# The row maxima of a pair attention: one transpose and four masked copies in place of four transposes and one copy

## The chip, the core and the metric

The kernel runs on one core of a Trainium2 chip. A core has five engines with instruction queues of their own: TensorE (PE; its weight loads are shown as PEld), VectorE (DVE), ScalarE (ACT), GpSimd (POOL) and SyncE (SP), which only starts transfers here. They meet through semaphores. SBUF is the core's memory of 128 partitions, PSUM the smaller one that TensorE writes (8 banks of 512 float32 per partition). The metric is the device time of one execution in microseconds, as a median over several.

## The reference

Two layers on x of shape (2, 1024, 128), each adding an attention, a feed-forward, another attention and another feed-forward to x. Only the attentions over 16 heads of 64 are touched. In one layer's terms:

```python
x = x + _L0_attn_a_ref(_layernorm(x), ...)   # no mask; one key and value head shared by all
x = x + _L0_ffn_ref(_layernorm(x), ...)      # both operands rounded to an FP6 grid
x = x + _L0_attn_b_ref(_layernorm(x), ...)   # causal, keys and values per head
x = x + _L0_ffn_ref(_layernorm(x), ...)
x = x + _L1_attn_a_ref(_layernorm(x), ...)   # causal, keys and values from a latent of 32
x = x + _L1_ffn_ref(_layernorm(x), ...)      # 8 experts, top 2, and a shared one
x = x + _L1_attn_b_ref(_layernorm(x), ...)   # causal, with biases
x = x + _L1_ffn_ref(_layernorm(x), ...)
```

and one attention is

```python
sim = jnp.einsum('bnhk,bmk->bnhm', q, k) / jnp.sqrt(KEY_DIM)
attn = jax.nn.softmax(sim, axis=-1)
o = jnp.einsum('bnhm,bmv->bnhv', attn, v)
out = jnp.einsum('bnhv,dhv->bnd', o, output_proj)
```

## The kernel before, in words

The program is a row of phases. `stream_phase` holds the first two attentions (the non-causal one from 75 to about 760 us, the causal one to about 1410) with the norm and feed-forward between them woven in; `latent_phase` is the third attention and has its own code, which the change doesn't touch; `attention_phase` is the last one (2010 to 2590). The first two and the last are "pair attentions": an item is one batch and two heads, head 0 on partitions 0 to 63 and head 1 on 64 to 127. An item has two units, its halves of 512 queries (`part` or `s`), and a unit has steps, one for each tile of 128 keys. There are 32 items in the stream and 16 in the last attention, so 96 units.

The softmax subtracts the row maximum before the exponential, and the scores are laid out with keys on partitions and queries along the free dimension. So the maxima are found first, from scores in the other layout:

- `chunk` (TensorE, L1010 and L530) makes scores with 128 queries on partitions, up to 512 keys of both heads, in PSUM banks 4 and 5.
- `row_max` (VectorE, L1210 and L697) reduces them to two numbers per partition, negated. Where a tile of queries has over 512 keys, the two halves go to `half_max`, and after the unit's last chunk a TENSOR_TENSOR takes their minimum into `neg_max` (L1217, L704). Where it has not, they go straight to `neg_max`. The buffer `neg_max` holds, for each half, four tiles of 128 columns, zero but for columns 0 and 64 of each, the two heads.
- `top` (TensorE, L1060 and L570) transposes the four tiles into the four quarters of PSUM bank 7, called `small`: the maxima of 512 queries now lie along the free dimension, on row 0 for head 0 and row 64 for head 1, zeros on all others.
- ScalarE copies the bank into `max_row` (L1146, L658).
- `scores` (TensorE, L986 and L989, L506 and L509) adds, to the product of keys and queries, the product of `pick` with `max_row`. The constant `pick` has ones in rows 0 and 64, so it spreads the maxima over the 128 keys.
- ScalarE takes the exponential (L1114, L621), GpSimd adds the tiles of it up (`add_up`, L1371, L781), TensorE multiplies with the values (`mix_step`, L1029, L549), and from the sums comes "total" (L1064, L574), a matmul with ones into the same bank `small`; VectorE inverts and multiplies (L1230, L1238), and "out" (L1069, L582) projects into `small` again.

The order is written out by hand. Every engine walks the steps `g` in pairs; `when` says at which step each use of `small` stands. Each use on TensorE first waits until the one before it has been copied out (`small_out`), and `scores` of a unit's first step waits for the copy of its "top". In a non-causal item (16 steps) the uses stand at 14 (top of half 0, for the next item), 1, 2, 3, 4, 6 (top of half 1), 10 and 11. In a causal item (12 steps) they stand at every step but two, and each top (steps 6 and 2) is followed at the very next step by a "total", with two calls of `mix_step` between them. Chunks run ten steps ahead of the scores.

Of the kernel before, what the change touches and what calls it, by code (L numbers as in the profile page):

```python
# [27 lines left out]
P = 128  # L28
# [53 lines left out]
def setup_phase(nc, m, a, dram):  # L82

    with phase(nc) as (ctx, sem):
# [40 lines left out]
        @block.gpsimd  # L125
        def _(pool):
            pool.memset(m.ident[:], 0.0).then_inc(zeroed, 1)
            pool.memset(a.shifted_ident[:], 0.0).then_inc(zeroed, 1)
            pool.memset(a.causal[:], 0.0).then_inc(zeroed, 1)
            pool.memset(m.earlier[:], 1.0).then_inc(zeroed, 1)  # L130
            pool.memset(ones, 1.0).then_inc(zeroed, 1)
            pool.memset(rows_of_ones, 0.0).then_inc(zeroed, 1)
            pool.memset(m.ones_row[:], 1.0).then_inc(zeroed, 1)
            pool.memset(a.ones[:], 1.0).then_inc(zeroed, 1)
            pool.memset(a.neg_max[:], 0.0).then_inc(zeroed, 1)
            pool.wait_ge(zeroed, 9)
            pool.affine_select(out=m.ident[:], in_=m.ident[:], compare_op=ALU.not_equal, fill=1.0, base=0,
                               pattern=[[-1, P]], channel_multiplier=1).then_inc(consts, 1)
            pool.affine_select(out=m.earlier[:], in_=m.earlier[:], compare_op=ALU.is_gt, fill=0.0, base=0,
                               pattern=[[1, EXPERTS], [-1, EXPERTS]], channel_multiplier=0).then_inc(consts, 1)  # L140
            for n, half in enumerate((slice(0, HD), slice(HD, P))):
                pool.wait_ge(consts, 2 + 3 * n)
                pool.affine_select(out=rows_of_ones[half], in_=rows_of_ones[half], compare_op=ALU.not_equal,
                                   fill=1.0, base=0, pattern=[[0, P]], channel_multiplier=1).then_inc(consts, 1)
                pool.affine_select(out=a.shifted_ident[half], in_=a.shifted_ident[half], compare_op=ALU.not_equal,
                                   fill=1.0, base=0, pattern=[[HD, 2], [-1, P]], channel_multiplier=1)\
                    .then_inc(consts, 1)
                pool.affine_select(out=a.causal[half], in_=a.causal[half], compare_op=ALU.is_ge, fill=MASKED, base=0,
                                   pattern=[[HD, 2], [-1, P]], channel_multiplier=1).then_inc(consts, 1)

            rows = (slice(0, LOW), slice(LOW, LOW + EXPERTS))
            done = 8
            for base, sign in ((0, 1), (ED - 1, -1)):
                for part in rows:
                    pool.wait_ge(consts, done)
                    pool.affine_select(out=ones[part], in_=ones[part], compare_op=ALU.is_ge, fill=0.0, base=base,
                                       pattern=[[sign, EXPERTS * ED]], channel_multiplier=-sign * ED)\
                        .then_inc(consts, 1)  # L160
                    done += 1
# [221 lines left out]
def attention_phase(nc, m, a, tag, dram, after, causal, biased=False, shared=False):  # L383
# [5 lines left out]
    with phase(nc) as (ctx, new_sem):  # L389
# [106 lines left out]
        def _(pe):  # L496
# [57 lines left out]
            def use_small(n, kind, i, part):  # L554
# [11 lines left out]
                                                w.v[:, 0 if shared else i // B, :], start=True, stop=True)  # L566
                elif kind == "top":
                    pe.wait_ge(max_ready, unit(i, part) + 1)
                    for t in range(TPG):
                        last = nc.tensor.transpose(small[:, t * P:(t + 1) * P], a.neg_max[:, part, t, :], m.ident[:])  # L570
                elif kind == "total":
                    pe.wait_ge(summed, sums_done[end_step(i, part) - 1])
                    for head, rows in enumerate(HEADS):
# [37 lines left out]
        def _(act):  # L611
# [19 lines left out]
            def take_small(n, kind, i, part):  # L631
# [23 lines left out]
                elif kind == "top":  # L655
                    if i >= 1:
                        act.wait_ge(scored, end_step(i - 1, part))
                    last = act.activation(a.max_row[:, part, :], small, ACT.Copy)  # L658
                else:
                    if unit(i, part) >= 1:  # L660
                        act.wait_ge(inverted, QUARTERS * unit(i, part))
                    last = act.activation(a.total[:], small, ACT.Copy)  # L662
# [19 lines left out]
        def _(dve):  # L682
            v = nc.vector

            def row_max(c):
# [3 lines left out]
                if split_max[s]:  # L689
                    out = a.half_max[:, part, t % TPG, :]  # L690
                    if part == 0 and t % TPG == 0 and unit(i, s) > 0:
                        dve.wait_ge(max_ready, unit(i, s))
                else:
                    out = a.neg_max[:, s, t % TPG, 0:P:HD]
                    if t % TPG == 0 and i >= 1:
                        dve.wait_ge(small_mm, use_of["top", i - 1, s] + 1)
                last = v.tensor_reduce(out, chunk_ps[:, :, 0:hi - lo], AX.X, ALU.max, negate=True)  # L697
                last.then_inc(maxed, 1)
                if c % NS == last_chunk[s]:
                    if split_max[s]:  # L700
                        if i >= 1:
                            dve.wait_ge(small_mm, use_of["top", i - 1, s] + 1)
                        dve.wait_ge(maxed, c + 1)
                        v.tensor_tensor(a.neg_max[:, s, :, 0:P:HD], a.half_max[:, 0], a.half_max[:, 1], ALU.min)\  # L704
                            .then_inc(max_ready, 1)
                    else:
                        dve.wait_ge(maxed, c + 1)
# [83 lines left out]
def shape_constants(nc, pool, a, sem):  # L791


    blank, shaped = sem("blank"), sem("shaped")
    for buffer, value in ((a.later[:], 0.0), (a.tri_scores[:], 0.0), (a.tri_chunk[:], 0.0), (a.unit32[:], 0.0), (a.pick4_raw, 0.0)):
        pool.memset(buffer, value).then_inc(blank, 1)
    pool.wait_ge(blank, 5)
    for rows in (slice(0, HD), slice(HD, P)):
        pool.affine_select(out=a.later[rows], in_=a.later[rows], compare_op=ALU.is_ge, fill=MASKED, base=0,
                           pattern=[[-HD, 2], [1, P]], channel_multiplier=-1).then_inc(shaped, 1)  # L800
    pool.wait_ge(shaped, 2)
    for rows in QUADRANTS:
        pool.affine_select(out=a.tri_scores[rows], in_=a.tri_scores[rows], compare_op=ALU.is_ge, fill=MASKED, base=0,
                           pattern=[[LATENT, 4], [-1, P]], channel_multiplier=1).then_inc(shaped, 1)
# [3 lines left out]
                           pattern=[[-1, LATENT]], channel_multiplier=1).then_inc(shaped, 1)  # L808
        pool.affine_select(out=a.pick4_raw[rows], in_=a.pick4_raw[rows], compare_op=ALU.not_equal, fill=1.0, base=0,
                           pattern=[[0, P]], channel_multiplier=1).then_inc(shaped, 1)  # L810
    pool.wait_ge(shaped, 18)
    pool.tensor_copy(a.pick4[:], a.pick4_raw).then_inc(shaped, 1)


def stream_phase(nc, m, a, dram, after):
# [6 lines left out]
    with phase(nc) as (ctx, new_sem):  # L822
# [153 lines left out]
        def _(pe):  # L976
# [73 lines left out]
            def use_small(n, kind, i, part):  # L1050
# [5 lines left out]
                    last = values(i, part)  # L1056
                elif kind == "top":
                    pe.wait_ge(max_ready, unit(i, part) + 1)
                    for t in range(TPG):
                        last = nc.tensor.transpose(small[:, t * P:(t + 1) * P], a.neg_max[:, part, t, :], m.ident[:])  # L1060
                elif kind == "total":
                    pe.wait_ge(summed, sums_done[end_step(i, part) - 1])
                    for head, rows in enumerate(HEADS):
# [40 lines left out]
        def _(act):  # L1104
# [19 lines left out]
            def take_small(n, kind, i, part):  # L1124
# [18 lines left out]
                elif kind == "top":  # L1143
                    if i >= 1:
                        act.wait_ge(scored, end_step(i - 1, part))
                    last = act.activation(a.max_row[:, part, :], small, ACT.Copy)  # L1146
                elif kind == "total":
                    if unit(i, part) >= 1:
                        act.wait_ge(inverted, QUARTERS * unit(i, part))
# [43 lines left out]
        def _(dve):  # L1193
# [3 lines left out]
            def row_max(c):  # L1197
# [6 lines left out]
                    if part == 0 and t % TPG == 0 and unit(i, s) > 0:  # L1204
                        dve.wait_ge(max_ready, unit(i, s))
                else:
                    out = a.neg_max[:, s, t % TPG, 0:P:HD]
                    if t % TPG == 0 and i >= 1:
                        dve.wait_ge(small_mm, use_of["top", i - 1, s] + 1)
                last = v.tensor_reduce(out, chunk_ps[:, :, 0:hi - lo], AX.X, ALU.max, negate=True)  # L1210
# [2 lines left out]
                if ends and split:  # L1213
                    if i >= 1:
                        dve.wait_ge(small_mm, use_of["top", i - 1, s] + 1)
                    dve.wait_ge(maxed, c + 1)
                    v.tensor_tensor(a.neg_max[:, s, :, 0:P:HD], a.half_max[:, 0], a.half_max[:, 1], ALU.min)\  # L1217
                        .then_inc(max_ready, 1)
                elif ends:
                    dve.wait_ge(maxed, c + 1)  # L1220
# [678 lines left out]
def build(nc, dram, out):  # L1899
    with ExitStack() as ctx:  # L1900
# [34 lines left out]
        a.unit32 = sb("unit32", [P, LATENT], BF16)  # L1935
        a.pick4_raw, a.pick4 = m.scratch[:, 7 * S:7 * S + P], sb("pick4", [P, P], F32R)
        a.later = sb("later", [P, 2, P], BF16)
        a.half_max = sb("half_max", [P, 2, TPG, 2])
        a.max_row = sb("max_row", [P, 2, BANK], F32R)
        a.mixed_raw = sb("mixed_raw", [P, 2, BANK])  # L1940
# [67 lines left out]
```

## Time and profile before

| | us |
|---|---|
| median of 3 timed runs | 2740.98 (2740.84 to 2741.83) |
| profiled execution | 2724.3 |
| its span | 2722.6 |
| TensorE busy | 2496.9 (92%) |
| VectorE busy | 1702.5 (63%) |
| ScalarE busy | 1159.5 (43%) |
| GpSimd busy | 1238.3 (45%) |

The span is from the first to the last instruction of the profiled execution; the time of the execution holds 1.7 us more around it. Shares are over the whole span, and the stages differ: the page's 40 slices show TensorE at nine tenths or more in all slices but those at the start and around the norms and feed-forwards. The mean granted clock of TensorE is 0.957 of full speed. Matmuls are pipelined and their ends are modelled, so that starts are the safer numbers for them.

### The profile page before, as it was taken

How to read it: one execution, taken by the hardware profiler on the slowest of the kernel's cores; microseconds unless marked ns; L12 is line 12 of the kernel's file. 1: busy time of each engine (PE TensorE's matmuls, PEld its weight loads, DVE VectorE, ACT ScalarE, POOL GpSimd, SP SyncE). 2: the span in 40 equal slices, each digit the busy share in tenths (PEclk: the TensorE clock that was granted, in tenths of full speed). 3: DMA queues.
4: the chain of work that ended last, by engine and by line, in shares of the span. 5: the costliest groups of instructions: out<-in, count | busy, mean ns of one | idle time of the engine just before them, and what ended most of it. 6: DMA issues, size and time to landing. Idle time of an engine off the chain costs nothing. (4 is left out here: it accounts for less than half of the span.)

```text
span 2722.6 us, 48683 instructions
## 1 busy us (share of the span) xinstructions
PE 2496.9 (92%) x20217; PEld 1321.3 (49%) x20217; DVE 1702.5 (63%) x2156; ACT 1159.5 (43%) x1526; POOL 1238.3 (45%) x809
## 2 busy tenths in 40 slices
PE   4999999999999999999994799997869999999969
PEld 2344444344444454555552566665535555555535
DVE  2577767877765766666657476764435566666644
ACT  2444444445444435444442244444124444444432
POOL 2577777766775535555550000000005455555520
PEclk9999999999999999999995799998879999999979
DMA  4000000000000000000000000000000000000000
GB/s 106 1 1 1 0 1 1 1 1 1 1 1 10 1 1 1 1 1 1 1 1 11 21 3 3 3 3 2 0 1 1 1 1 1 1 1 1 1 0 16
DMA packets 19183, 14.08 MB, mean 5 GB/s; under 512 B 3090, under 2 KB 17811, under 8 KB 18836
## 3 DMA queue, kind: packets, MB, share of 16 engines
q1 hardware_dynamic: 18964, 10.97, 1.6%
q8 instruction: 161, 2.64, 0.4%
q14 instruction: 58, 0.48, 0.1%
HBM read 9.39 MB, written 1.57 MB: 4 GB/s over the span
## 5 line engine op out<-in xcount | busy, mean ns | idle before, releaser
L1371 POOL TENSOR_TENSOR sums<-sums,p 128x1024 f32<-128x1024 f32 (+3 forms) x384 | 815.3, 2123 | 386.0 <-PE ps L1029 344.1
L1210 DVE TENSOR_REDUCE half_max<-ps 128x2 f32<-128x1024 f32 (+3 forms) x384 | 439.6, 1145 | 330.3 <-PE ps L1010 317.9
L1114 ACT ACTIVATE p<-ps 128x1024 f32<-128x1024 f32 (+3 forms) x384 | 347.5, 917 | 212.2 <-PE ps L989 153.0
L986 PE MATMUL ps<-q,k 64*128 64x512 f32 (+3 forms) x1792 | 425.2, 553 | 0.0
L781 POOL TENSOR_TENSOR sums<-sums,p 128x1024 f32<-128x1024 f32 (+3 forms) x160 | 277.1, 1732 | 198.5 <-PE ps L549 182.1
L1029 PE MATMUL ps<-p,v 128*64 128x512 f32 (+3 forms) x1536 | 338.7, 555 | 0.0
L989 PE MATMUL ps<-max_row,pick 64*128 64x512 f32 (+3 forms) x896 | 325.6, 723 | 0.0
L1230 DVE RECIPROCAL inverse<-total 128x128 f32<-128x128 f32 x256 | 239.9, 940 | 15.9 <-ACT total L1150 12.3
L1010 PE MATMUL ps<-k_near,q_near 64*128 64x512 f32 (+2 forms) x896 | 199.8, 442 | 40.0 <-DVE half_max L1210 39.9
L697 DVE TENSOR_REDUCE half_max<-ps 128x2 f32<-128x1024 f32 (+3 forms) x128 | 129.3, 1010 | 123.1 <-PE ps L530 109.3
L1590 ACT ACTIVATE p<-ps 128x2048 f32<-128x2048 f32 (+1 forms) x80 | 136.6, 1708 | 161.7 <-PE ps L1493 90.7
L1010 PEld LDWEIGHTS ps<-k_near,q_near 64*128 64x128 f32 x896 | 85.3, 187 | 246.2 <-issue 148.3
L986 PEld LDWEIGHTS ps<-q,k 64*128 64x128 f32 x1792 | 161.9, 187 | 55.9 <-issue 40.9
L1029 PEld LDWEIGHTS ps<-p,v 128*64 128x64 f32 x1536 | 97.0, 137 | 177.7 <-issue 112.4
L1643 DVE TENSOR_REDUCE quarter_max<-ps 128x2 f32<-128x1024 f32 (+3 forms) x128 | 128.2, 1012 | 59.8 <-PE ps L1517 34.2
L506 PE MATMUL ps<-q,k 64*128 64x512 f32 (+3 forms) x768 | 163.6, 504 | 0.0
L621 ACT ACTIVATE p<-ps 128x1024 f32<-128x1024 f32 (+3 forms) x160 | 118.7, 768 | 68.5 <-PE ps L514 52.0
L717 DVE RECIPROCAL inverse<-total 128x128 f32<-128x128 f32 x128 | 119.6, 940 | 15.8 <-ACT total L662 12.3
L989 PEld LDWEIGHTS ps<-max_row,pick 64*128 64x128 f32 x896 | 85.1, 187 | 89.8 <-issue 84.7
L1705 POOL TENSOR_TENSOR mixed<-mixed_raw,inverse 128x256 f32<-128x256 f32 x32 | 23.3, 727 | 229.7 <-DVE inverse L1661 229.7
L509 PE MATMUL ps<-max_row,pick 64*128 64x512 f32 (+3 forms) x384 | 121.5, 629 | 0.0
L549 PE MATMUL ps<-p,v 128*64 128x512 f32 (+3 forms) x640 | 115.7, 474 | 0.0
(252 smaller groups left out, 3990.9 us busy)
## 6 DMA issues: line engine op xcount, KB each, us to landing
q_w<-in_wq SPq DMA_DIRECT2D x3, 512.0 KB
o_w<-in_wo SPq DMA_DIRECT2D x3, 512.0 KB
k_w<-in_wk SPq DMA_DIRECT2D x2, 512.0 KB
v_w<-in_wv SPq DMA_DIRECT2D x2, 512.0 KB
out<-x SPq DMA_DIRECT2D x4, 256.0 KB, 2.9
scratch<-in_wq_t SPq DMA_DIRECT2D x1, 512.0 KB, 5.4
scratch<-in_w_out SPq DMA_DIRECT2D x1, 512.0 KB, 7.7
gate<-in_gate SPq DMA_DIRECT2D x1, 320.0 KB
```

The source lines that it names most:

```text
L506: nc.tensor.matmul(out[:, head, 0:width], a.k[rows, key_slot(i, 3), k * P:(k + 1) * P], a.q[rows, i % 3, s * BANK + lo:(s + 1) * BANK], st ...
L697: last = v.tensor_reduce(out, chunk_ps[:, :, 0:hi - lo], AX.X, ALU.max, negate=True)
L781: pool.tensor_tensor(sums, sums, probabilities(g)[:, :, lo:BANK], ALU.add).then_inc(summed, 1)
L986: nc.tensor.matmul(out[:, head, 0:width], a.k[rows, owner(i) % 3, k * P:(k + 1) * P], a.q[rows, i % 3, s * BANK + lo:(s + 1) * BANK], star ...
L989: last = nc.tensor.matmul(out[:, head, 0:width], a.pick[rows, :], a.max_row[rows, s, lo:BANK], start=False, stop=not diagonal)
L1010: last = nc.tensor.matmul(chunk_ps[:, head, 0:hi - lo], a.q_near[rows, i % 2, t * P:(t + 1) * P], a.k_near[rows, owner(i) % 2, lo:hi], sta ...
L1029: last = nc.tensor.matmul(mix[rows, lo:BANK], a.v[:, owner(i) % 2, k, value_columns(i, head)], probabilities(g)[:, head, lo:BANK], start=k ...
L1114: act.activation(probabilities(g)[:, :, lo:BANK], score[g % 2][:, :, 0:BANK - lo], ACT.Exp)\
L1210: last = v.tensor_reduce(out, chunk_ps[:, :, 0:hi - lo], AX.X, ALU.max, negate=True)
L1230: v.reciprocal(a.inverse[:, cols], a.total[:, cols]).then_inc(inverted, 1)
L1371: pool.tensor_tensor(sums, sums, probabilities(g)[:, :, lo:BANK], ALU.add).then_inc(summed, 1)
L1590: act.activation(probs[:, g % SLOTS, :, 0:width(s, n)], score[:, :, 0:width(s, n)], ACT.Exp)\
```

## The change

Four things are changed, in both pair phases alike.

- `neg_max`: the maxima of tile t now go to columns t and 64 + t of the first tile alone, so one transpose gives rows 0 to 3 (head 0) and 64 to 67 (head 1), each row the maxima of one tile.
- The spreading: ScalarE makes four copies of the same 128 columns, one into each quarter of `max_row`, with the scale taken from column t of a new constant `row_mask` [128 x 4], which is 1 on rows t and 64 + t and 0 elsewhere. All other rows become 0.
- `pick` has ones in rows 0 to 3 and 64 to 67, where only the row of the right tile is not zero.
- The minimum of the halves is a TENSOR_REDUCE over the last axis of one reordered view of `half_max`, in place of a TENSOR_TENSOR of its two halves.

```diff
@@ setup_phase
-                pool.affine_select(out=rows_of_ones[half], in_=rows_of_ones[half], compare_op=ALU.not_equal,
-                                   fill=1.0, base=0, pattern=[[0, P]], channel_multiplier=1).then_inc(consts, 1)
+                pool.affine_select(out=rows_of_ones[half], in_=rows_of_ones[half], compare_op=ALU.is_ge,
+                                   fill=1.0, base=-TPG, pattern=[[0, P]], channel_multiplier=1).then_inc(consts, 1)
@@ use_small, on TensorE (stream_phase; attention_phase has the same)
                     pe.wait_ge(max_ready, unit(i, part) + 1)
-                    for t in range(TPG):
-                        last = nc.tensor.transpose(small[:, t * P:(t + 1) * P], a.neg_max[:, part, t, :], m.ident[:])
+                    last = nc.tensor.transpose(small[:, 0:P], a.neg_max[:, part, 0, :], m.ident[:])
@@ take_small, on ScalarE
                     if i >= 1:
                         act.wait_ge(scored, end_step(i - 1, part))
-                    last = act.activation(a.max_row[:, part, :], small, ACT.Copy)
+                    for t in range(TPG):
+                        last = act.activation(a.max_row[:, part, t * P:(t + 1) * P], small[:, 0:P], ACT.Copy,
+                                              scale=a.row_mask[:, t:t + 1])
@@ row_max, on VectorE
-                    out = a.neg_max[:, s, t % TPG, 0:P:HD]
+                    out = a.neg_max[:, s, 0, t % TPG:P:HD]
...
-                    v.tensor_tensor(a.neg_max[:, s, :, 0:P:HD], a.half_max[:, 0], a.half_max[:, 1], ALU.min)\
+                    v.tensor_reduce(a.neg_max[:, s, 0, :].rearrange("p (h t) -> p t h", h=2)[:, 0:TPG, :],
+                                    a.half_max[:].rearrange("p a t h -> p t h a"), AX.X, ALU.min)\
                         .then_inc(max_ready, 1)
@@ shape_constants, on GpSimd, at the start of the stream
-    for buffer, value in ((a.later[:], 0.0), (a.tri_scores[:], 0.0), ...
+    for buffer, value in ((a.row_mask[:], 0.0), (a.later[:], 0.0), (a.tri_scores[:], 0.0), ...
...
     for rows in (slice(0, HD), slice(HD, P)):
+        pool.affine_select(out=a.row_mask[rows], in_=a.row_mask[rows], compare_op=ALU.not_equal, fill=1.0, base=0,
+                           pattern=[[-1, TPG]], channel_multiplier=1).then_inc(shaped, 1)
@@ build
+        a.row_mask = sb("row_mask", [P, TPG])
```

No instruction changes its place among the others; the counts at a top do. On TensorE, around a top in the non-causal part (line numbers of the changed kernel differ by a few). Before, and then changed:

```order
L1010 MATMUL ps<-k_near,q_near 128x512 x2
L1060 MATMUL ps<-ident,neg_max 128x128 x4
L1029 MATMUL ps<-p,v 64x512 x4
L1010 MATMUL ps<-k_near,q_near 128x512 x2
L986 MATMUL ps<-q,k 128x512 x2
```

```order
L1014 MATMUL ps<-k_near,q_near 128x512 x2
L1063 MATMUL ps<-ident,neg_max 128x128
L1033 MATMUL ps<-p,v 64x512 x4
L1014 MATMUL ps<-k_near,q_near 128x512 x2
L990 MATMUL ps<-q,k 128x512 x2
```

Behind the top stand the mixes and the next chunk. Where four transposes stood there is one; the chunk ahead of it, the mixes behind it and the chunk and scores that follow are the same. On ScalarE, around a top in the non-causal part, before and then changed:

```order
L1114 ACTIVATE p<-ps 128x1024 x2
L1146 ACTIVATE max_row<-ps 128x512
L1114 ACTIVATE sums<-ps 128x1024
L1114 ACTIVATE p<-ps 128x1024
L1122 ACTIVATE mixed_raw<-ps 128x512
```

```order
L1117 ACTIVATE p<-ps 128x1024 x2
L1150 ACTIVATE max_row<-ps,row_mask 128x128 x4
L1117 ACTIVATE sums<-ps 128x1024
L1117 ACTIVATE p<-ps 128x1024
L1125 ACTIVATE mixed_raw<-ps 128x512
```

The copy of 512 columns has become four of 128 that read `row_mask` too, in the same place between the exponentials of two units.

## Rows read from the trace of the kernel before

**Rows 1.** busy time by stage: us, then each engine (instructions); PEclk, DMA share, GB/s
```profile
75.00:1410.00 1335.00, 1293.32 (x7814) 609.84 (x7816) 916.23 (x986) 619.65 (x811) 856.06 (x472) 0.99 0.01 1
2070.00:2560.00 490.00, 486.35 (x3606) 254.51 (x3602) 306.06 (x339) 227.84 (x327) 267.68 (x194) 1.00 0.00 1
```

**Rows 2.** TensorE's waits (total, times, longest) in 90:480, 480:640, 640:800
```profile
PE ps L1010 <- DVE half_max L1210: 3.6, 7, 0.5
...
PE ps L1010 <- DVE half_max L1210: 10.4, 10, 2.5
...
PE ps L1010 <- DVE half_max L1210: 1.6, 3, 0.5
```

**Rows 3.** order of time, TensorE, 299 to 303: start, us, engine, line, shapes [idle]
```profile
299.48 0.49 PE L1010 MATMUL ps<-k_near,q_near 64*128 64x512 f32 x2 [0.52 <-DVE half_max L1210]
299.90 0.66 PE L1060 MATMUL ps<-ident,neg_max 128*128 128x128 f32 x4
...
302.69 0.59 PE L986 MATMUL ps<-q,k 64*128 64x512 f32 x2
```

**Rows 4.** order of time, ScalarE, from 324
```profile
324.19 0.59 ACT L1146 ACTIVATE max_row<-ps 128x512 fp32r<-128x512 f32 x1
```

**Rows 5.** order of time, TensorE, four windows of 0.02 us from 323.38
```profile
323.38 0.33 PE L1060 MATMUL ps<-ident,neg_max 128*128 128x128 f32 x1
...
323.55 0.38 PE L1060 MATMUL ps<-ident,neg_max 128*128 128x128 f32 x2
...
323.76 0.27 PE L1060 MATMUL ps<-ident,neg_max 128*128 128x128 f32 x1
323.97 0.65 PE L1029 MATMUL ps<-p,v 128*64 128x512 f32 x2
```

**Rows 6.** order of time, TensorE, a causal item, 1206 to 1210
```profile
1206.72 0.66 PE L1060 MATMUL ps<-ident,neg_max 128*128 128x128 f32 x4
...
1209.08 0.60 PE L1064 MATMUL ps<-sums,ones 128*64 128x512 f32 x2
```

**Rows 7.** order of time, TensorE, the next item, 1230 to 1233
```profile
1230.58 0.66 PE L1060 MATMUL ps<-ident,neg_max 128*128 128x128 f32 x4
...
1232.71 0.60 PE L1064 MATMUL ps<-sums,ones 128*64 128x512 f32 x2
```

**Rows 8.** order of time, ScalarE, 1205 to 1208
```profile
1205.61 2.12 ACT L1114 ACTIVATE p<-ps 128x1024 f32<-128x1024 f32 x2 [0.92 <-PE ps L989]
1207.62 0.59 ACT L1146 ACTIVATE max_row<-ps 128x512 fp32r<-128x512 f32 x1
```

**Rows 9.** three lines of ScalarE: ns min/median/max, first and last start
```profile
L198 ACT ACTIVATE ffn_wt<-ps x1: 258/258/258, 23.1 to 23.1; 128x128 f32<-128x128 f32 x1
...
L643 ACT ACTIVATE k<-ps,qk_bias x32: 687/687/688, 2013.8 to 2546.4; 128x512 f32<-128x512 f32 x32
...
L351 ACT ACTIVATE scratch<-x,shift_n,rstd_n x48: 477/479/494, 35.5 to 2628.0; 128x128 f32<-128x128 f32 x48
```

**Rows 10.** order of time, TensorE and ScalarE, 391 to 395
```profile
393.91 1.77 PE L1046 MATMUL ps<-v_w,xn_t 128*128 128x64 f32 x14 [0.79 <-ACT max_row L1146]
...
393.27 0.59 ACT L1146 ACTIVATE max_row<-ps 128x512 fp32r<-128x512 f32 x1
```

**Rows 11.** one line of VectorE, the minimum: ns min/median/max, first and last start
```profile
L1217 DVE TENSOR_TENSOR neg_max<-half_max x48: 172/1328/1655, 73.8 to 1403.6; 128x8 f32<-128x8 f32 x48
```

**Rows 12.** order of time, VectorE, 295 to 300
```profile
295.85 1.64 DVE L1217 TENSOR_TENSOR neg_max<-half_max 128x8 f32<-128x8 f32 x1
...
298.27 1.15 DVE L1210 TENSOR_REDUCE half_max<-ps 128x2 f32<-128x1024 f32 x1
```

**Rows 13.** order of time, GpSimd and VectorE, 504 to 506
```profile
503.80 2.37 POOL L1371 TENSOR_TENSOR sums<-sums,p 128x1024 f32<-128x1024 f32 x1
...
505.40 0.63 DVE L1293 TENSOR_REDUCE scratch<-scratch 128x16 f32<-128x512 f32 x1
```

**Rows 14.** order of time, GpSimd, 54 to 56
```profile
54.92 0.61 POOL L1361 CAST q_near<-q 128x512 fp32r<-128x512 f32 x1 [1.90 <-ACT q L1129]
```

More of the change, by code:

```diff
@@ L794, in shape_constants @@
     blank, shaped = sem("blank"), sem("shaped")
-    for buffer, value in ((a.later[:], 0.0), (a.tri_scores[:], 0.0), (a.tri_chunk[:], 0.0), (a.unit32[:], 0.0), (a.pick4_raw, 0.0)):
+    for buffer, value in ((a.row_mask[:], 0.0), (a.later[:], 0.0), (a.tri_scores[:], 0.0), (a.tri_chunk[:], 0.0), (a.unit32[:], 0.0), (a.pick4_raw, 0.0)):
         pool.memset(buffer, value).then_inc(blank, 1)
-    pool.wait_ge(blank, 5)
+    pool.wait_ge(blank, 6)
     for rows in (slice(0, HD), slice(HD, P)):
+        pool.affine_select(out=a.row_mask[rows], in_=a.row_mask[rows], compare_op=ALU.not_equal, fill=1.0, base=0,
+                           pattern=[[-1, TPG]], channel_multiplier=1).then_inc(shaped, 1)
         pool.affine_select(out=a.later[rows], in_=a.later[rows], compare_op=ALU.is_ge, fill=MASKED, base=0,
                            pattern=[[-HD, 2], [1, P]], channel_multiplier=-1).then_inc(shaped, 1)
-    pool.wait_ge(shaped, 2)
+    pool.wait_ge(shaped, 4)
     for rows in QUADRANTS:
@@ L810, in shape_constants @@
                            pattern=[[0, P]], channel_multiplier=1).then_inc(shaped, 1)
-    pool.wait_ge(shaped, 18)
+    pool.wait_ge(shaped, 20)
     pool.tensor_copy(a.pick4[:], a.pick4_raw).then_inc(shaped, 1)
@@ L1058, in use_small @@
                     pe.wait_ge(max_ready, unit(i, part) + 1)
-                    for t in range(TPG):
-                        last = nc.tensor.transpose(small[:, t * P:(t + 1) * P], a.neg_max[:, part, t, :], m.ident[:])
+                    last = nc.tensor.transpose(small[:, 0:P], a.neg_max[:, part, 0, :], m.ident[:])
                 elif kind == "total":
@@ L1145, in take_small @@
                         act.wait_ge(scored, end_step(i - 1, part))
-                    last = act.activation(a.max_row[:, part, :], small, ACT.Copy)
+                    for t in range(TPG):
+                        last = act.activation(a.max_row[:, part, t * P:(t + 1) * P], small[:, 0:P], ACT.Copy,
+                                              scale=a.row_mask[:, t:t + 1])
                 elif kind == "total":
@@ L1206, in row_max @@
                 else:
-                    out = a.neg_max[:, s, t % TPG, 0:P:HD]
+                    out = a.neg_max[:, s, 0, t % TPG:P:HD]
                     if t % TPG == 0 and i >= 1:
@@ L1216, in row_max @@
                     dve.wait_ge(maxed, c + 1)
-                    v.tensor_tensor(a.neg_max[:, s, :, 0:P:HD], a.half_max[:, 0], a.half_max[:, 1], ALU.min)\
+                    v.tensor_reduce(a.neg_max[:, s, 0, :].rearrange("p (h t) -> p t h", h=2)[:, 0:TPG, :],
+                                    a.half_max[:].rearrange("p a t h -> p t h a"), AX.X, ALU.min)\
                         .then_inc(max_ready, 1)
```

## The prediction

> **What bounds the kernel now.** I read the busy time per stage first. In the two pair attentions of the stream (75 to 1410 us, non-causal up to about 760) TensorE is busy 1293 of 1335 us, in the last attention (2070 to 2560) 486 of 490 [rows 1]. The granted clock is 0.99 and 1.00 there, the upper of its two levels (2.4 GHz). These stretches hold nearly all of the 96 places of the change: 16 non-causal pairs of heads, 16 causal ones in the stream and 16 causal ones at the end, two halves (units) each. So TensorE sets the pace, and work taken off it should come off the end, unless a wait replaces it. The waits of TensorE come second: the only one of weight is `chunk` (L1010) on VectorE's row maximum. It is 3.6 us over 90 to 480 (7 waits of 0.52), 10.4 us over 480 to 640, where VectorE quantises beside the attention, and 1.6 us over 640 to 800 [rows 2].
>
> The third view is the time order around a "top". Within a non-causal unit TensorE waits 0.52 us for VectorE, does four transposes at 299.90, and comes to the scores that read `max_row` at 302.69, 2.79 us later [rows 3]. ScalarE copies 0.81 us after the transposes began (323.38 to 324.19), since it is still in an exponential; the copy lasts 0.59 [rows 4, 5]. It is done 1.4 us before it is needed, so it is hidden now. In a causal half the next use of the same PSUM bank, "total" (L1064), comes much sooner: 1206.72 to 1209.08 for the top of half 0, and 1230.58 to 1232.71 for that of half 1 [rows 6, 7]. That is where a longer copy would show.
>
> **The transposes.** Four start at 323.38, 323.55, 323.66 and 323.76 (the row at 323.55 holds two, 0.38 us in all where one takes 0.27, so 0.11 apart), and the next matmul at 323.97 [rows 5]: intervals of 0.17, 0.11, 0.11 and 0.20 us, 0.59 together. What a lone one takes up to the next matmul isn't in the trace. From below it is one inner interval, 0.11, which saves 0.48; from above it keeps the long first record (0.33 against 0.27) and the long last interval, 0.20 + 0.06 = 0.26, which saves 0.33. I take 0.33, as the first and the last interval have reasons (an uncovered weight load, a change of tile shape) that stay. 96 x 0.33 = 31.7 us off TensorE.
>
> **The copies.** One ACTIVATE of 128x512 becomes four of 128x128, each with a pointer (`row_mask`) as scale. A 128x128 one from PSUM without a pointer took 258 ns. A 128x512 takes 0.59 to 0.60 us without a pointer [rows 4, 8] and 0.687 with one (L643, its bias), so one pointer is +0.09. That gives 0.35 us. ACTIVATEs in a row overlap: the pair of exponentials runs 1205.61 + 2.12 = 1207.73 and the copy starts at 1207.62, 0.11 before that [rows 8]; I take 0.10. So four take 3 x 0.25 + 0.35 = 1.10 us, against 0.59. Bounds: no price for a pointer, 3 x 0.16 + 0.26 = 0.74; the price of the 128x128 with two pointers from SBUF, 479 ns, 3 x 0.38 + 0.48 = 1.62 [rows 9].
> The Trainium skill, "ScalarE: Activation LUTs", section "What ACT_TABLE_LOAD costs", gives 186 ns + 0.833 per element, about 93 ns for each pointer operand, and an overlap of about 93 ns between neighbours. The pointer and the overlap agree with the rows; the base doesn't quite (293 by the page, 258 in the row, which reads PSUM). An estimate by the page alone is 1.27 us for the four, and the sum below would be 4 to 5 us smaller.
>
> Where do 0.5 us more on ScalarE show? Queued behind the copies are the next exponentials, which wait for scores that come later, and TensorE's next use of the bank `small`.
> - Non-causal: copies from 324.19 to 325.29, the scores at 323.38 + 2.79 - 0.33 = 325.84. Nothing.
> - Causal, half 0: ScalarE is free at 1207.62 whatever TensorE saves, so the last copy ends at 1208.72; TensorE starts 0.05 us after a copy that it waits for (393.27 + 0.59, then 393.91) [rows 10], so 1208.77. "total" would now be due at 1209.08 - 0.33 = 1208.75, and its weight load, otherwise done ahead, is uncovered by some 0.06 (again 0.33 against 0.27). I take 0.1 us of new wait in each of 32 such units: -3.2 us.
> - Causal, half 1: ScalarE waits for the transpose here; the lone one ends 0.33 after 1230.58, copies to 1232.01, "total" due at 1232.38. Nothing.
> - Where another use of the bank stands right behind the copy, TensorE waits for it today already (393.91, 0.79 us of idle [rows 10]) and would wait 0.5 us longer and lose the 0.33: two or three places, -2 us.
>
> **The minimum.** L1217 took 172 ns at best, 1328 in the median, 1655 at worst [rows 11]; the short ones are where GpSimd was idle. At 295.85 it took 1.64, and the reduce that TensorE waits for followed at 298.27, ended at 299.42, and released the chunk at 299.48 [rows 3, 12]. As a TENSOR_REDUCE with one SBUF source it should stay near the 0.17: a TENSOR_REDUCE from SBUF at 505.40 took 0.63 us for 512 elements right inside a GpSimd sum of 503.80 to 506.17, about half of the 1.15 of 1024 elements [rows 12, 13]. Then the reduce ends 1.4 us earlier and the 0.52 us wait is gone, ten times in 90 to 480 and 640 to 800: +5 us. In 480 to 640 six minima give VectorE back about 1 us each, but its other two-operand work still waits for GpSimd; of the 10.4 us I take 4, bounds 0 and 8. In the causal parts the minimum mostly falls where GpSimd rests, so nothing. The chance against it is that the reduce, too, waits for GpSimd.
> The Trainium skill, "SBUF — State Buffer", section "Who interferes with whom", says that a VectorE instruction with two SBUF inputs contends with a GpSimd one that reads SBUF, and that `tensor_reduce` never does on this chip. Row 505.40 agrees.
>
> **The rest.** GpSimd makes `row_mask` in three more small instructions at the start; its cast at 54.92 had been idle for 1.90 us before [rows 14], which hides them. `pick` with four rows of ones has the same shape. The order of all else is unchanged.
>
> **Sum.** 31.7 - 3.2 - 2 + 9 = 35.5 us. The profiled execution took 2724.3 us (span 2722.6 and 1.7 around it), so 2689 for a profile of the changed kernel. The median of the timed runs is 2741.0, 16.7 above the profiled one; the terms are the same there, so 2705.5. A change is one that can be told if it is over 0.2%, 5.5 us.
>
> **Rivals.**
> 1. *More than forecast.* A lone transpose costs an inner interval (96 x 0.48 = 46), no new wait at "total", and VectorE's relief is whole (5 + 8): 46 + 13 - 2 = 57 us, 2684. For it: VectorE's and TensorE's waits feed each other in 480 to 640. Against: the uncovered first weight load.
> 2. *The minimum still waits for GpSimd.* 9 us less: 2714.5. For it: it is the part of the change whose row is of another shape.
> 3. *Copies at the two-pointer price*, 1.62 us for four. Causal half 0: 1207.62 + 1.62 + 0.05 = 1209.29, 0.21 later than today; half 1: 1230.91 + 1.67 = 1232.58, 0.13 earlier; 32 x (-0.21 + 0.13) = -2.6; non-causal 32 x 0.33 = 10.6; with 9 and -2 that is 15 us: 2726. Then the saving moves from TensorE into a wait of L1064 on L1146.
> 4. *Slower.* The four copies don't overlap and cost 0.48 each, 1.92 us. "total" of half 0 comes 1207.62 + 1.97 - 1209.08 = 0.51 late, of half 1 0.17 late, 32 x 0.68 = 22; the non-causal halves give 5, the minimum 9, the close followers take 2: +10, 2751. The point from which it is slower is 1.8 us for the four copies. For it: they all read the same PSUM columns. Against: the exponentials overlap, and the rows price one pointer at 0.09.
>
> **How the numbers follow.** Forecast 0.54 (its own range 2697 to 2713), rival 1 0.12, rival 2 0.12, rival 3 0.10, rival 4 0.05, something unseen that eats all of it 0.07. The range is to leave out no more than 2 in 10: 2685 to 2727, which takes in rival 3 and nearly rival 1. Faster 0.88, within 0.2% 0.06, slower 0.06.
>
> **What would show it.** In the changed profile: next matmul 0.26 us after a transpose (0.11 or 0.20 speaks for rival 1); copies in fours, 0.35 us each and 1.10 from first start to last end; L1064's counterpart waiting for the copy by about 0.1 us, 32 times (rival 3: 0.5); the minimum at 0.17 to 0.2 us everywhere, and the 0.52 us waits of `chunk` gone between 90 and 480. The prediction is wrong if TensorE's idle time in the three stretches grows by more than 10 us, or if its busy time there falls by less than 25.

## The result

The changed kernel takes 2699.43 us (median of 4 runs, 2697.23 to 2704.23), the kernel before 2740.91 (2738.26 to 2741.83): a ratio of 0.9854, 95% interval 0.9838 to 0.9871, or 41.5 us less. The forecast was 2705.5. The profiled execution of the changed kernel took 2697.2 us, a span of 2695.5, only 27.1 below that of before. Medians are over the fast executions: one of `old_min` below took 3423.9 us at a mean granted clock of 0.67 and isn't counted. Why the profiles are closer than the medians is the larger part of what follows.

From the page, and the busy time of the stretches that hold the same work as those of [rows 1]:

```profile
PE 2473.1 (92%) x19929; PEld 1293.8 (48%) x19929; DVE 1683.6 (62%) x2156; ACT 1210.4 (45%) x1814; POOL 1241.2 (46%) x812
```
```profile
75.00:1392.60 1317.60, 1279.85 (x7622) 594.46 (x7624) 898.35 (x986) 653.01 (x1003) 858.00 (x472) 0.99 0.01 1
2052.50:2534.10 481.60, 477.98 (x3517) 245.55 (x3513) 304.55 (x338) 241.61 (x406) 266.94 (x194) 1.00 0.00 1
```

The first row counts 192 matmuls less than [rows 1], three for each of 64 units. The two stretches are 17.4 and 8.4 us shorter, 21.8 us of it busy time of TensorE and 4.0 idle time.

**The lone transpose.** TensorE in order of time (start, us, engine, line, shapes, [idle]), a top of half 1 and one of half 0, answering [rows 5] and [rows 3]:

```profile
318.06 0.33 PE L1063 MATMUL ps<-ident,neg_max 128*128 128x128 f32 x1
318.32 1.08 PE L1033 MATMUL ps<-p,v 128*64 128x512 f32 x4
```
```profile
294.57 0.40 PE L1014 MATMUL ps<-k_near,q_near 64*128 64x512 f32 x2
294.90 0.33 PE L1063 MATMUL ps<-ident,neg_max 128*128 128x128 f32 x1
295.15 1.94 PE L1033 MATMUL ps<-p,v 128*64 128x512 f32 x8
```

The next matmul starts 0.26 us after the transpose, where it started 0.59 after the first of four. Ahead of the second top the chunk has no idle time in brackets: the 0.52 us of [rows 3] is gone.

**The copies.** ScalarE in order of time, and its line's durations (min/median/max in ns), answering [rows 4]:

```profile
318.86 1.14 ACT L1150 ACTIVATE max_row<-ps,row_mask 128x128 fp32r<-128x128 f32 x4
```
```profile
L1150 ACT ACTIVATE max_row<-ps,row_mask x256: 359/371/397, 77.1 to 1389.4; 128x128 fp32r<-128x128 f32 x128
...
  PEld ps L1067: 16.0, 31
```

Four copies of 0.37 us take 1.14 us together. The last row names who waited for them most (us, times): the weight load of "total" 31 times. Its matmul waited once, 0.2 us. Around a causal top TensorE and ScalarE show, answering [rows 6 to 8]:

```profile
1192.66 0.33 PE L1063 MATMUL ps<-ident,neg_max 128*128 128x128 f32 x1
...
1194.75 0.65 PE L1067 MATMUL ps<-sums,ones 128*64 128x512 f32 x2
```
```profile
1193.56 1.14 ACT L1150 ACTIVATE max_row<-ps,row_mask 128x128 fp32r<-128x128 f32 x4
```
```profile
1216.31 0.33 PE L1063 MATMUL ps<-ident,neg_max 128*128 128x128 f32 x1
...
1218.13 0.60 PE L1067 MATMUL ps<-sums,ones 128*64 128x512 f32 x2
```

From top to "total" half 0 takes 2.09 us (2.36 before), half 1 1.82 (2.13). The copies of half 0 end at 1194.70 (1193.56 + 1.14) and "total" starts at 1194.75.

**The minimum and TensorE's waits**, answering [rows 11, 2, 10]: the line of the minimum; the only row of waits of TensorE in 90:470, and that of `chunk` in 470:630; and one place in order of time.

```profile
L1222 DVE TENSOR_REDUCE neg_max<-half_max x48: 171/173/175, 73.7 to 1386.6; 128x8 f32<-128x16 f32 x48
```
```profile
PE ps L1050 <- ACT max_row L1150: 1.7, 1, 1.7
```
```profile
PE ps L1014 <- DVE half_max L1215: 9.7, 9, 3.2
```
```profile
387.53 1.66 PE L1050 MATMUL ps<-v_w,xn_t 128*128 128x64 f32 x13 [1.66 <-ACT max_row L1150]
```

The minimum is at 0.17 us in all 48 places, and the seven waits of `chunk` in the first stretch are gone. In the second one, where VectorE quantises, 9.7 us are left of 10.4. The values' matmul behind a top (0.79 us of wait before) now waits 1.66.

### The profile page after: what moved, and what is told of

Read it like the earlier page. It is cut to its first block and busy times, and to the rows that moved or that the text cites. A ratio compares the mean times of both kernels' runs of the same rounds, so it can differ in the third digit from the quotient of the medians.

```text
span 2695.5 us, 48400 instructions
## 1 busy us (share of the span) xinstructions
PE 2473.1 (92%) x19929; PEld 1293.8 (48%) x19929; DVE 1683.6 (62%) x2156; ACT 1210.4 (45%) x1814; POOL 1241.2 (46%) x812
## 5 line engine op out<-in xcount | busy, mean ns | idle before, releaser
L990 PEld LDWEIGHTS ps<-q,k 64*128 64x128 f32 x1792 | 162.8, 187 | 57.1 <-issue 41.5
L1711 POOL TENSOR_TENSOR mixed<-mixed_raw,inverse 128x256 f32<-128x256 f32 x32 | 23.3, 729 | 229.9 <-DVE inverse L1667 229.9
```

The costliest lines, as they stand in the source:

```text
L990: nc.tensor.matmul(out[:, head, 0:width], a.k[rows, owner(i) % 3, k * P:(k + 1) * P], a.q[rows, i % 3, s * BANK + lo:(s + 1) * BANK], star ...
```

## The experiments

Each kernel was timed beside the kernel before on the same chip; "before" is the median there.

### The two kernels again

`after_again` and `after_c` are the changed kernel, `before_b` the kernel before, all with no edit.

> The changed kernel once more, as the yardstick of this set. Theory: it is 36 to 42 us below the kernel before in the timed runs. The two profiled executions so far lie only 27 us apart (2724.3 and 2697.2), while the timed medians lie 41.5 apart; if the 14 us between are a property of the one profiled execution of the kernel before, this profile lies within a few us of its own timed median (about 2699). If they are a property of profiled executions as such, it lies some 14 us below.

2705.3 us (2699.15 to 2707.06, 5 runs), before 2740.4; ratio 0.9874 (0.9855 to 0.9893). That is 35.1 below, 1 us short of the 36 to 42. The profiled execution took 2707.1, close to the median of its own kernel, so the 14 us belong to the one profiled execution of before.

> The kernel before once more, for a profile of it at its usual time. Its one profiled execution took 2724.3 us and 21 timed ones 2727 to 2744, with nearly all at 2737 to 2744. Theory: the execution of 2724.3 was one in which TensorE's clock came back earlier around 1425 to 1560 us (two stretches of half clock of 61 and 34 us there, against one of 123 in the four other profiles, which is worth 10 us), so this profile shows one long stretch of half clock there, and is about 2734 or more; what is left up to 2740 shows as more half clock elsewhere. Rival: the pair attentions themselves take longer in it, by 10 us or more between 108 and 1430 us, through longer waits for VectorE.

One execution: 2744.8 us, span 2743.1, against 2724.3 for the first profile. Busy time by stretch, columns as in [rows 1], of the first profile of before, of `before_b`, of the first one of after and of `after_again`:

```profile
900.00:1080.00 180.00, 166.06 (x1178) 86.55 (x1176) 123.82 (x156) 79.43 (x122) 92.74 (x64) 0.97 0.00 1
1410.00:1530.00 120.00, 67.35 (x342) 38.95 (x338) 68.27 (x173) 26.32 (x48) 18.27 (x15) 0.63 0.07 18
1530.00:1650.00 120.00, 116.96 (x2340) 80.33 (x2342) 81.66 (x101) 57.51 (x54) 10.94 (x16) 0.97 0.01 3
```
```profile
900.00:1080.00 180.00, 166.33 (x1128) 86.83 (x1124) 116.78 (x150) 77.45 (x119) 84.47 (x58) 0.92 0.00 1
1410.00:1530.00 120.00, 75.71 (x380) 43.60 (x376) 65.03 (x171) 29.98 (x53) 21.78 (x17) 0.63 0.07 18
1530.00:1650.00 120.00, 108.64 (x1953) 72.37 (x1952) 74.61 (x89) 47.82 (x47) 8.74 (x13) 0.86 0.01 2
```
```profile
1410.00:1530.00 120.00, 65.01 (x494) 40.80 (x494) 70.36 (x175) 25.97 (x45) 6.29 (x9) 0.60 0.07 18
1530.00:1650.00 120.00, 119.91 (x2396) 82.15 (x2398) 82.71 (x103) 57.88 (x53) 11.08 (x16) 1.00 0.01 3
```
```profile
1410.00:1530.00 120.00, 65.19 (x340) 39.49 (x342) 65.21 (x170) 21.79 (x41) 6.18 (x9) 0.52 0.07 18
1530.00:1650.00 120.00, 119.92 (x2346) 81.53 (x2344) 81.10 (x99) 57.14 (x53) 10.31 (x15) 0.97 0.01 3
```

The granted clock has two levels, 1.2 and 2.4 GHz, so a stretch at 0.63 spent 0.37 x 120 / 0.5 = 89 us at the lower one. Over 1410 to 1650 the four profiles were at the lower level for 96, 122, 96 and 122 us. In all four the level fell behind the last "total" of the stream, in a wait of 4.9 us for `mixed`; a wait of 2.8 us for the sums stood ahead of it and one of 21 us for the norm behind. In the first profile of before it fell at 1431, was back from 1493 to 1503 and again from 1537; in `before_b` it fell at 1441 and was back at 1564 only. From the last "total" of the stream to the last latent chunk, start to start, it is 430.9 and 441.1 us in the two profiles of before, 431.3 and 441.2 in those of after: the same code gives 10 us away or not. The stretch 900 to 1080, the norms woven into the causal attention, differs too (0.97 and 0.92), 7.6 us over its sixteen units. The first profile of before had the better of both. Of 56 timed runs of it nine took under 2730 us and 44 over 2737. So half of the 20.5 us between these two profiles is the clock behind the stream. The rest is mostly in the norm stretches, and there too it is the clock, as the theory had it ("more half clock elsewhere"): 0.92 instead of 0.97 over 180 us is 18 us more at the lower level, worth up to 9. The rival wanted longer waits for VectorE; those of `chunk` in the stream are 39.9 and 40.9 us.

`before_b` and `after_again` are alike behind the stream: 2743.1 - 2705.3 = 37.8 us. In the stretches of [rows 1] they have:

```profile
75.00:1420.20 1345.20, 1302.89 (x7814) 615.25 (x7816) 915.30 (x986) 619.41 (x811) 855.50 (x472) 0.99 0.01 1
2090.50:2580.50 490.00, 486.34 (x3606) 254.54 (x3602) 305.89 (x339) 227.74 (x327) 267.48 (x194) 1.00 0.00 1
```
```profile
75.00:1392.40 1317.40, 1279.61 (x7622) 594.56 (x7624) 898.03 (x986) 652.20 (x1003) 857.12 (x472) 0.99 0.01 1
2062.50:2544.20 481.70, 478.07 (x3517) 245.46 (x3513) 304.47 (x338) 241.44 (x406) 266.44 (x194) 1.00 0.00 1
```

TensorE's busy time falls by 23.3 + 8.3 = 31.6 us here and its idle time by 4.5. Up to about 3 us of the busy time are clock again: over 900 to 1080 `after_again` has 0.94, `before_b` 0.92.

> The changed kernel as it is, for comparison on the same chip and for a further profile: 2699 to 2705.

2698.05 us (2696.47 to 2701.89, 5 runs), before 2741.92; ratio 0.985 (0.9826 to 0.9875): 1 us under the 2699 to 2705.

### One part alone

`four_turns`, the changed kernel with four transposes, of which the copies read only the first:

```diff
-                    last = nc.tensor.transpose(small[:, 0:P], a.neg_max[:, part, 0, :], m.ident[:])
+                    for t in range(TPG):
+                        last = nc.tensor.transpose(small[:, t * P:(t + 1) * P], a.neg_max[:, part, t, :], m.ident[:])
```

> The changed kernel with four transposes per unit again: the other three turn columns that the copies don't read, so the result is the same. Theory: TensorE sets the pace, each transpose more costs it 0.11 us, 96 x 0.33 = 31 us above the changed kernel, plus 96 x up to 0.1 to 0.5 in the causal halves, as the copies then start later in one half: 2731 to 2735. Rival (the transposes were partly hidden behind waits, and the gain is in the copies or the minimum): less than 20 us above.

2729.75 us (2721.15 to 2735.72, 12 runs), before 2740.4; ratio 0.9965 (0.9952 to 0.9977). That is 24.5 over `after_again` in the medians and 27.1 in the spans (2732.4), 0.28 us a unit. TensorE in order of time:

```profile
1371.43 0.66 PE L1065 MATMUL ps<-ident,neg_max 128*128 128x128 f32 x4
1372.01 1.08 PE L1034 MATMUL ps<-sums,v 128*64 128x512 f32 x4
```

The 0.58 is back, and from top to "total" it is 2.35 us in half 0 again. The rival's "under 20" falls; the theory's 31 to 35 was too high, for it added a wait of the copies to the 31, where the later "total" takes one away.

`old_min`, the changed kernel with the old minimum (L705 the same), and `min_only`, the kernel before with the new one:

```diff
-                    v.tensor_reduce(a.neg_max[:, s, 0, :].rearrange("p (h t) -> p t h", h=2)[:, 0:TPG, :],
-                                    a.half_max[:].rearrange("p a t h -> p t h a"), AX.X, ALU.min)\
+                    v.tensor_tensor(a.neg_max[:, s, 0, :].rearrange("p (h t) -> p t h", h=2)[:, 0:TPG, :],
+                                    a.half_max[:, 0], a.half_max[:, 1], ALU.min)\
```
```diff
-                    v.tensor_tensor(a.neg_max[:, s, :, 0:P:HD], a.half_max[:, 0], a.half_max[:, 1], ALU.min)\
+                    v.tensor_reduce(a.neg_max[:, s, :, 0:P:HD], a.half_max[:].rearrange("p a t h -> p t h a"), AX.X, ALU.min)\
```

> The changed kernel with the minimum as a TENSOR_TENSOR of two SBUF operands again; one transpose and four masked copies stay. Theory (the parts add up): 5 to 9 us above the changed kernel, median 2704 to 2708, with the 0.5 us waits of chunk back in the non-causal items. Rival (a faster TensorE makes the minimum matter more, since chunk comes 0.33 us earlier): 10 to 14 us above.

2712.17 us (2699.99 to 2716.61, 5 runs), ratio 0.9895 (0.9872 to 0.9918): 6.9 over `after_again`, as expected. The minimum, and TensorE's waits in 90:480 and 480:640:

```profile
L1222 DVE TENSOR_TENSOR neg_max<-half_max x48: 172/1308/1642, 72.5 to 1395.9; 128x8 f32<-128x8 f32 x48
```
```profile
PE ps L1014 <- DVE half_max L1215: 3.6, 7, 0.5
```
```profile
PE ps L1014 <- DVE half_max L1215: 11.3, 11, 2.4
```

> The kernel before with only the minimum changed to a TENSOR_REDUCE of one SBUF operand (same output columns, four transposes, one copy). Theory (the minimum no longer waits for GpSimd, and only the non-causal part has a chunk waiting behind it): 5 us in steady non-causal items (ten waits of 0.5 to 0.7 us gone) and 0 to 4 where VectorE quantises, so 2 to 9 us below the kernel before; the minimum 0.17 us everywhere. Rival (the reduce waits for GpSimd too, or VectorE had slack): within 2 us of the kernel before.

2716.99 us (2710.23 to 2723.76, 6 runs), ratio 0.9918 (0.9897 to 0.994): 23 us, where 2 to 9 were expected. The same rows of it:

```profile
L1217 DVE TENSOR_REDUCE neg_max<-half_max x48: 171/173/176, 70.5 to 1389.2; 128x8 f32<-128x16 f32 x48
```
```profile
PE ps L1010 <- DVE half_max L1210: 0.4, 1, 0.4
```
```profile
PE ps L1010 <- DVE half_max L1210: 8.4, 7, 3.2
```

Against the profile `before_b`, 24.6 us longer, it is 1.9 shorter in the start, 11.9 in the non-causal part, 10.9 in the sixteen units of the causal part into which the norms are woven, and the same elsewhere. Against the first profile of before, the non-causal part is 9.1 shorter. The waits of `chunk` in the stream fall from 40.9 (39.9) to 33.1 us. The 10.9 are the clock, which in this stretch was

```profile
900.00:1080.00 180.00, 167.93 (x1229) 89.14 (x1228) 120.45 (x157) 81.03 (x122) 87.66 (x63) 0.99 0.00 1
```

0.99 against 0.92: some 25 us less at the lower level, worth up to 13. Nothing shows that the minimum brings that: `after_again` and `old_min`, which differ in it alone, both have 0.94 there. In the last attention, where the clock is the same, the minimum is worth nothing. Its transposes in `before_b`, `min_only`, `after_again` and `old_min` (the last numbers are the first and last start):

```profile
L570 PE MATMUL ps<-ident,neg_max x128: 272/273/473, 2051.9 to 2606.8; 128*128 128x128 f32 x128
L570 PE MATMUL ps<-ident,neg_max x128: 272/273/473, 2027.2 to 2582.2; 128*128 128x128 f32 x128
L569 PE MATMUL ps<-ident,neg_max x32: 328/329/474, 2024.3 to 2570.4; 128*128 128x128 f32 x32
L569 PE MATMUL ps<-ident,neg_max x32: 328/329/474, 2033.7 to 2579.9; 128*128 128x128 f32 x32
```

That is 554.9, 555.0, 546.1 and 546.2 us for 31 units (0.3 less in the first two, whose last start is that of the fourth transpose). The two undoings are worth 24.5 and 6.9 in the medians, the minimum alone 23, all together 35: medians of this kernel move by several us with the clock and don't add.

`no_mask`, the changed kernel with the masking left out:

```diff
-                        last = act.activation(a.max_row[:, part, t * P:(t + 1) * P], small[:, 0:P], ACT.Copy,
-                                              scale=a.row_mask[:, t:t + 1])
+                        last = act.activation(a.max_row[:, part, t * P:(t + 1) * P], small[:, 0:P], ACT.Copy)
```

> The changed kernel with the four copies without row_mask as scale (plain copies, so all four rows go to every quarter of max_row: this leaves out the masking, and the maxima that are subtracted are sums over four tiles). It prices the pointer operand. Theory: each copy goes from 0.37 to 0.26 or 0.28 us, the four from 1.14 to about 0.75, and the 0.06 us that total waits in one causal half of each of 32 items goes: 2 to 4 us below the changed kernel (2705 in the last set), no more, because the copies are hidden elsewhere. Rival (ScalarE has become a limit with these copies): over 8 us.

2703.19 us (2697.84 to 2704.02, 5 runs), before 2739.54; ratio 0.9868 (0.9843 to 0.9892). The copies:

```profile
L1149 ACT ACTIVATE max_row<-ps x256: 270/285/325, 76.7 to 1384.4; 128x128 fp32r<-128x128 f32 x128
```

The pointer costs 371 - 285 = 86 ns. In half 0 "total" comes 2.03 us behind the top instead of 2.09: 0.06 is the wait that the pointers add. Its four matmuls also take 1.03 us instead of 1.08, so that the chunk behind it starts 2.98 us after the top in `no_mask`, 3.10 in after and 3.31 in before. TensorE in order of time, a half 0 of `no_mask`, of after (whose top is at 1192.66) and of before (top at 1206.72, [rows 6]):

```profile
1188.50 0.33 PE L1062 MATMUL ps<-ident,neg_max 128*128 128x128 f32 x1
1190.53 1.03 PE L1066 MATMUL ps<-sums,ones 128*64 128x512 f32 x4
1191.48 0.50 PE L1013 MATMUL ps<-k_near,q_near 64*128 64x512 f32 x2
```
```profile
1194.75 1.08 PE L1067 MATMUL ps<-sums,ones 128*64 128x512 f32 x4
1195.76 0.50 PE L1014 MATMUL ps<-k_near,q_near 64*128 64x512 f32 x2
```
```profile
1210.03 0.50 PE L1010 MATMUL ps<-k_near,q_near 64*128 64x512 f32 x2
```

From the first to the last transpose the last attention takes 544.6 us in `no_mask`, 1.5 less than in `after_again`: 0.1 for each item, which has one half 0. The median, 2.1 us below that of `after_again` in another set, can't tell 2 to 4 from nothing; the rival's "over 8" falls.

### The clock behind the stream

Both kernels were given idle matmuls, whose product nobody reads, while TensorE waits for a norm: 28 ahead of the first pair of transposes of a norm with a feed-forward, 8 ahead of the others, 5 at each further pair:

```diff
+            def fill(count, bank):
+                for _ in range(count):
+                    nc.tensor.matmul(m.ps[:, bank, :], m.ident[:], m.gate[:, 0:BANK], start=True, stop=True)
+
+            fill(28 if linear else 8, 0)
...
+                    if pair:
+                        fill(5, 3)
```

> The changed kernel, plus matmuls into PSUM banks that nobody reads at the start of each norm phase (28 of 128x512 where the norm holds a feed-forward, then 5 more before its second pair, 8 in the other norms), where TensorE waits 8 to 21 us for ScalarE or VectorE. Theory: the timed runs differ by whether TensorE's clock comes back early or late around 1425 to 1560 us, since TensorE is idle there; kept at work it stays at the full level, the long stretch of half clock goes, and the kernel is 10 to 25 us faster than the changed one (2680 to 2695), with a smaller spread of runs. Rival (the half clock there follows something else than TensorE's idle time, or the added matmuls delay the work behind them): no faster than the changed kernel, or slower by up to 15 us.

> The kernel before with the same added matmuls. Theory: the timed gap between the two kernels (35 to 41 us so far) holds 0 to 5 us from the norms' clock and the rest from the pair attentions, so the two filled kernels lie 30 to 38 us apart. Rival (a large part of the timed gap is the clock of the norm phases, which differs between the two by chance of position): they lie under 27 us apart, as the first two profiles did.

`fill_after` took 2700.92 us (2698.84 to 2702.43, 6 runs), not 2680 to 2695, and no less than `after_c` beside it (2698.05), as its rival had it; `fill_before` 2734.63 (2733.08 to 2741.73, 12 runs); before took 2741.92. The ratios are 0.9855 (0.9831 to 0.9879) and 0.9985 (0.9967 to 1.0002). The two are 33.7 us apart, inside the expected 30 to 38. Then with fewer, placed better:

```diff
-            fill(28 if linear else 8, 0)
+            fill(21 if linear else 7, 0)
...
-                        fill(5, 3)
+                        fill(4, 3)
...
+            if linear:
+                fill(6, 7)
```

> The changed kernel with the added matmuls cut to the waits they stand in: 21 instead of 28 ahead of the first pair (they ran 6 us past the point where VectorE was ready), 4 instead of 5 ahead of the second, 6 new ones into bank 7 ahead of the last transposes (the 5.5 us wait for ScalarE after which the clock fell at 1475), 7 in the other norms. Theory: the 6 us of overrun go, and the clock is at its upper level when the latent attention begins, worth another 3 to 8: 2686 to 2694, and the spread stays within 5 us. Rival (the clock falls in the following short waits anyway): 2692 to 2698, just the overrun.

> The changed kernel on the same chip in the same set: 2698 to 2705.

`fill2_after` took 2686.04 us (2684.46 to 2687.38, 4 runs), ratio 0.9811 (0.9783 to 0.984); `after_d`, the changed kernel beside it, 2703.3 (2692.87 to 2705.61, 5 runs), ratio 0.9869 (0.9838 to 0.99); before 2740.3. So `fill2_after` is 17 us under the changed kernel beside it, inside the expected 2686 to 2694; `after_d` is inside its own range. TensorE in order of time, and busy time by stretch, of `fill_after` and then `fill2_after`:

```profile
1420.23 27.09 PE L284 MATMUL ps<-gate,ident 128*128 128x512 f32 x56 [1.59 <-PEq L62]
1447.16 1.04 PE L279 MATMUL ps<-ident,scratch 128*128 128x128 f32 x8
```
```profile
1470.00:1530.00 60.00, 42.95 (x281) 25.00 (x283) 18.29 (x22) 11.79 (x18) 4.31 (x7) 0.50 0.14 36
```
```profile
1416.41 21.06 PE L284 MATMUL ps<-gate,ident 128*128 128x512 f32 x42 [1.59 <-PEq L62]
1437.30 1.04 PE L279 MATMUL ps<-ident,scratch 128*128 128x128 f32 x8
```
```profile
1470.00:1530.00 60.00, 44.35 (x532) 27.65 (x532) 26.88 (x33) 15.13 (x19) 5.03 (x8) 0.72 0.14 36
```

The first fill held the real work up: it ended at 1447.16 against 1437.30, and 1470 to 1530 still fell wholly to the lower clock. With 21 the transposes start ten us earlier, 6 of them by the shorter fill and 3.8 because it started earlier, and the clock there is 0.72. Three counts were changed at once, so which of them brought the clock back isn't shown.

## Why the prediction was right, and where it wasn't

- **Transposes, 31.7 us: right.** The lone one takes 0.26 up to the next matmul, so 0.33 are saved. Rival 1's 0.48 falls. Undone alone they were worth 27.1 in the spans, against 28.5, the 31.7 less the 3.2 of the wait at "total", which goes with them.
- **Copies, 0.35 each and 1.10 for four: right** (0.37 and 1.14). A pointer was put at 0.09 and took 0.086. Rivals 3 and 4 (1.62 and 1.92) fall with it. The price of a copy without a pointer worked out from the Trainium skill, "ScalarE: Activation LUTs", section "What ACT_TABLE_LOAD costs" (an estimate of 293 ns), is closer to the 285 of `no_mask` than the row that I went by (258); the estimate of 1.27 us for the four by the same section is 0.13 too high.
- **Wait at "total", -3.2: right.** In half 0 the chunk behind "total" starts 3.10 us after the top instead of 3.31, so 0.21 of the 0.33 is left: 0.06 goes in the wait and 0.05 in longer matmuls of "total". Over the last attention it is 0.1 for each half 0, as forecast. Read the rows with care: the weight load is charged with 16.0 us in 31 waits, 0.5 each, which is what I had named as the sign of rival 3. A weight load that would have run ahead can wait 0.5 and hold its matmul up by 0.06; the interval between matmuls decides.
- **Close followers, -2: right.** The two values' matmuls behind a top wait 1.7 us each, 0.9 more than 0.8.
- **Minimum, +9: right for the sum, not in its parts.** The non-causal part of `min_only` is 9.1 and 11.9 us shorter than in the two profiles of before, the clock's share in it included. It is at 0.17 beside GpSimd everywhere, and the steady 5 came (`old_min` has its 3.6 us of waits back). The 4 us in 480 to 640 hardly came as waits of `chunk`: 10.4 became 9.7, and 8.4 in `min_only`. Rival 2 falls. The minimum's 171 to 175 ns agree with the rule of the Trainium skill, "SBUF — State Buffer", section "Who interferes with whom", that a `tensor_reduce` doesn't contend with GpSimd.
- **"In the causal parts [...] nothing": right.** The last attention takes 554.9 and 555.0 us with the old and the new minimum, and 546.2 and 546.1 in the changed kernel. The 10.9 us of `min_only` in the norm stretch go with the clock, 0.99 against 0.92; one and the same kernel varies there by 7.6 us.
- **The own time of the profile.** I took the sum from 2724.3 and set "the median 16.7 above, the terms are the same there". The terms were, but not for a reason that I had: that profile was a rare short execution. Against it the change shows 27.1, under my 35.5; between profiles alike behind the stream 37.8; between the filled kernels 33.7. The sign by which I would have been wrong, busy time falling by less than 25 us, did come in the first pair (21.8) and not in the second (31.6). It was a bad sign: busy time holds the clock, and the changed kernel's profile had 0.94 over 900 to 1080 where that of before had 0.97.

The medians differ by 41.5, 35.1, 43.9 and 37.0 us in the four comparisons, around the 35.5 and mostly above it. An estimate without the clock: if a us at the lower level costs half a us, a span times its mean granted clock is what it would take at the upper level. That gives 2722.6 x 0.957 - 2695.5 x 0.955 = 31 us for the first pair of profiles and 2743.1 x 0.949 - 2705.3 x 0.950 = 33 for the second; it counts too much where TensorE only waits. So the mechanism gives 31 to 33 us, slightly under the sum, and no term of the sum explains why the first medians lay 41.5 apart: that 2705.5 came within 6 us of 2699.4 is the sum and, in part, luck with the clock. Not settled is what decides, for one and the same kernel, whether the lower clock lasts 96 or 122 us, or how often it falls in the norms of the stream. The profiles of after (2695.5, 2705.3, and `after_d`) show both lengths too, so it isn't shown that the change favours one.

## What to carry to other kernels

Where maxima lie in a few columns of otherwise empty tiles, pack them before the transpose: TensorE gets 0.33 us a unit back and ScalarE pays 0.5. What that costs hangs on the next use of the same PSUM bank: nothing where it stood 1.8 us behind the top and the copies started at once, 0.1 where it stood 2.0 us behind and the copies started 0.9 late, 0.9 where it stood right behind them. A tiny VectorE operation with two SBUF operands can take 1.6 us beside GpSimd, and as a reduce of one operand 0.17. Before a sum is set against a profiled execution, see where that stands among the timed runs; and a wait for a norm can hold idle matmuls, if they end when the real ones are due.

## What the runs showed of the hardware

- The same instructions, with TensorE waiting alike before them, got the upper clock back after 96 or after 122 us at the lower one: 10 us of 2700.
- A 128x512 idle matmul of f32 took 27.09 / 28 = 0.97 us across that stretch, at a clock that was partly the lower one (0.77 over 1410 to 1440).
- A 128x128 f32 transpose between other matmuls took 0.26 us to the next one, each further one of four 0.11 more.
- The VectorE minimum that gives 128x8 f32 took 172 ns at best, 1328 in the median and 1655 at worst with two SBUF operands, and 171 to 176 as a reduce of one.
- A pointer as scale cost a ScalarE copy of 128x128 from PSUM 86 ns (371 against 285).
